# A two-layer cross-attention kernel: the second layer walks the batches backwards, and three pieces of its set-up stand in another order

## The chip, the cores and the metric

One Trainium2 chip, one NeuronCore. The metric is the device time of one execution in microseconds. The engines are TensorE (PE in the rows; its weight loads are PEld), VectorE (DVE), ScalarE (ACT), GpSimd (POOL) and the queue of SyncE (SP), which issues nearly all DMAs. ACT issues a few too.

## The reference

Two cross-attention layers with residuals and an MLP, on x of 8 batches x 56 rows x 256 features. Both layers attend to the same context, 8 batches x 1500 positions x 256.

```python
B, Q, T, D, H, K, F = 8, 56, 1500, 256, 16, 128, 1024

def cross_attention(q_in, kv_in, wq, bq, wk, bk, wv, bv, wo, bo, bias_k, bias_v):
    qh = (q_in @ wq + bq).reshape(b, q_len, H, K)
    kh = (kv_in @ wk + bk).reshape(b, t, H, K)
    vh = (kv_in @ wv + bv).reshape(b, t, H, K)
    kh = concatenate([kh, broadcast(bias_k)], axis=1)   # one more key
    vh = concatenate([vh, broadcast(bias_v)], axis=1)
    weights = softmax(einsum("bqhk,bthk->bhqt", qh, kh) / sqrt(K))
    return einsum("bhqt,bthk->bqhk", weights, vh).reshape(b, q_len, H * K) @ wo + bo

x = x + cross_attention(layer_norm(x, ln1), ctx, ...layer 1...)
x = x + cross_attention(layer_norm(x, ln2), ctx, ...layer 2...)
h = layer_norm(x, ln_mlp)
return x + gelu(h @ w_fc1 + b_fc1) @ w_fc2 + b_fc2
```

## The kernel before

The key projection is moved onto the queries: instead of projecting 12,000 context rows for every head, each head's query is carried through its key weights, so that scores are a product of the context itself with `qt` (256 features, 448 rows x 16 heads). In the same way the softmax weights are applied to the context, and only the result goes through the value and output weights. The one extra key is handled by its own logit (`lb`), for which the "key-bias product" of a head, `g_prod`, multiplies its key weights with the difference `dk` of bias_k and bk, and a reduce sums it into `g_cols`.

Matmuls run on fp32r operands, each split into a high part and a low part (the difference of the value and its high part); a product is three matmuls, high x high, high x low, low x high. So everything that enters a matmul is split first: ACT or DVE makes the high part by a copy, GpSimd or DVE the low part by a subtraction. This holds for the weights (`w_raw` to `w`: `weight_hi` on ACT, `weight_lo` on GpSimd) and for the context: one batch of it is resident in `ctx`, once as rows (`nat`) and once transposed (`tr`), in 4 pieces each. A piece comes by DMA into `nat_stage` or `tr_stage`; `nat_part_hi` and `tr_part_hi` (DVE) and `nat_part_lo` and `tr_part_lo` (GpSimd) split it.

A layer has these stages:

1. Query stage, a loop over 16 heads in quads of four. For head h TensorE computes the query from the normalized rows (L650), ACT copies it out (`query_hi`, L955), DVE takes the difference (`query_lo`, L1222), TensorE carries it through the key weights (L671), ACT writes it to `qt` (L967). Four weight buffers rotate; SP's `load_weight` for head h+4 waits until DVE's product of head h has read its buffer (`gp_ready`) and GpSimd has made its low part. In the same loop the four pieces of batch 0's `nat` and `tr` are loaded and split.
2. Attention stage, a loop over 8 batches. Each batch has two groups (4 and 3 tiles of 128 rows and heads) of 12 chunks of 125 positions: scores (L682), running maximum, shift, exp, split of the weights (L509), weighted context (L703 to L705), with the pieces of the next batch loaded and split as those of this one are used up.
3. Output stage, again a loop over 16 heads: value weights (L650), the extra key's share (a mask `pm` on GpSimd, L568, and L727), output weights (L747). Its input `oth`, the context result of one head, is copied from `qt` in two parts for the first two heads: an early one for the tiles that are complete, a late one (`EARLY`, 3 tiles) for those of the last group.

Then the layer norm of the sum (`norm`: statistics, a chain of small steps from `ln_v` on, `xn`, transposes on TensorE, `ht`).

Every engine has its program written out by hand, in order, with semaphores between the engines. An instruction whose wait is not met holds all that stand behind it on its engine. The order around the change is thus the order of the code in each engine's block. At the start, SP sends `hrow` (rows for the key bias), the four row groups of x, the tables; after DVE's `hdiff`, the difference of two of these rows, it writes `dk_rows` to memory, sends `vrow`, two weight tiles and some tables, and then reads `dk_rows` back, spread over all partitions, as `dk_first` (heads 0 to 3) and `dk_rest`. ACT's queue sends the first two weight tiles.

Semaphore counts that run on over both layers are written as a multiple of the layer, for pieces `l * (B * PIECES)`.

## Time and profile before

| | |
|---|---|
| runs | 1279.06, 1282.16, 2014.25 us; median 1282.16 |
| profiled execution | 1280.71 us, span of its instructions 1278.9 us |
| mean granted TensorE clock | 0.996 |
| busy: TensorE, GpSimd, ScalarE, VectorE | 1252.2, 905.1, 807.2, 794.6 us |
| moved by DMA | 72.58 MB |

The span runs from the first to the last instruction of the core; 1.8 us of the execution lie around it. One of the three runs took much longer than the others. Busy times of engines overlap, so they don't add up to the span. A row of the timeline gives start, duration, engine, line, operation, the written tile, the read ones, shapes and count, and in brackets how long the engine stood idle before it and what ended that. Rows with a count merge several instructions.

### The profile page before, as it was taken

What the parts mean: (1) busy time and instruction counts of PE and PEld (TensorE: products, weight loads), DVE (VectorE), ACT (ScalarE), POOL (GpSimd) and SP (SyncE); (2) the same over time, 40 slices, a digit from 0 to 9 for tenths busy, and PEclk for the clock granted to TensorE, in tenths of its full rate; (3) what the DMA queues carried; (4) which work ended last, traced back from release to release, by engine and by line L of the source; (5) the groups of instructions that cost most, each with busy time, mean ns of one, the idle gap of its engine ahead of it and who ended that gap; (6) DMA issues with size and microseconds to landing.
All of it is one profiled execution on the core that took longest, in us unless ns stands there. A gap on an engine that the chain in (4) does not pass through costs nothing.

```text
span 1278.9 us, 26549 instructions
## 1 busy us (share of the span) xinstructions
PE 1252.2 (98%) x8140; PEld 1152.3 (90%) x8140; DVE 794.6 (62%) x1369; ACT 807.2 (63%) x1585; POOL 905.1 (71%) x750
## 2 busy tenths in 40 slices
PE   6999999999999999999999999999999999999998
PEld 6779999999999999998887999999999999999897
DVE  5745656566666666566785656666656666655654
ACT  4745666666656566676584656666666666666755
POOL 4737777777777777678673768686868686866882
PEclk9999999999999999999999999999999999999999
DMA  5401111111111111012331111111111111101131
GB/s 166 144 10 49 37 61 36 60 36 60 36 60 36 60 37 59 31 39 83 121 126 40 38 38 61 36 60 36 60 36 60 36 60 37 60 30 52 50 95 40
DMA packets 30670, 72.58 MB, mean 57 GB/s; under 512 B 3104, under 2 KB 4512, under 8 KB 30624
## 3 DMA queue, kind: packets, MB, share of 16 engines
q1 hardware_dynamic: 30336, 71.49, 18.1%
q8 instruction: 23, 0.38, 0.1%
q10 hardware_dynamic: 288, 0.52, 0.1%
q14 instruction: 23, 0.19, 0.0%
HBM read 71.52 MB, written 0.48 MB: 56 GB/s over the span
## 4 chain that ended last, share of the span: by engine, by line
PE 91%; DVE 4%; ACT 2%; issue 2%; DMA 0%; POOL 0%; DVEq 0%; ACTq 0%; SPq 0%; POOLq 0%
PE psum L682 36%; PE psum L703 13%; PE psum L704 13%; PE psum L705 13%; PE psum L650 5%; PE psum L747 4%; PE psum L714 2%; PE psum L671 2%; DVE g_prod L1193 1%; PE psum L689 1%; PE psum L696 1%; PE psum L600 1%; DVE qh L1222 1%; ACT on L994 1%; DMA w_raw<-weights 0%
## 5 line engine op out<-in xcount | busy, mean ns | idle before, releaser
L509 POOL TENSOR_TENSOR pt<-slots,pt 125x512 fp32r<-125x512 f32 (+1 forms) x384 | 446.4, 1168 | 216.5 <-ACT slots L988 184.9
L682 PE MATMUL psum<-qs,ctx 128*125 128x384 f32 (+1 forms) x2304 | 543.1, 372 | 1.3 <-ACT slots L1019 0.8
L682 PEld LDWEIGHTS psum<-qs,ctx 128*125 128x125 f32 x2304 | 396.4, 187 | 47.5 <-ACT slots L1019 8.3
L703 PE MATMUL psum<-ctx,pt 125*128 125x258 f32 x1344 | 385.5, 287 | 2.8 <-ACT on L994 2.7
L704 PE MATMUL psum<-ctx,pt 125*128 125x256 f32 x1344 | 379.3, 282 | 0.0
L705 PE MATMUL psum<-ctx,pt 125*128 125x258 f32 x1344 | 379.1, 282 | 0.0
L1281 DVE TENSOR_TENSOR t_max<-psum,t_max 125x512 f32<-125x512 f32 (+1 forms) x320 | 199.2, 622 | 261.2 <-PE psum L682 260.9
L987 ACT ACTIVATE pt<-slots 125x512 fp32r<-125x512 f32 (+1 forms) x384 | 221.1, 576 | 193.1 <-DVE slots L1269 178.6
L1019 ACT ACTIVATE slots<-psum 125x512 f32<-125x512 f32 (+1 forms) x384 | 207.0, 540 | 141.8 <-DVE t_max L1281 132.2
L703 PEld LDWEIGHTS psum<-ctx,pt 125*128 125x128 f32 x1344 | 253.4, 189 | 19.9 <-ACT on L994 12.7
L704 PEld LDWEIGHTS psum<-ctx,pt 125*128 125x128 f32 x1344 | 254.1, 189 | 6.0
L705 PEld LDWEIGHTS psum<-ctx,pt 125*128 125x128 f32 x1344 | 254.6, 189 | 0.0
L1269 DVE TENSOR_TENSOR slots<-slots,psum 125x512 f32<-125x512 f32 (+1 forms) x384 | 232.9, 611 | 19.2 <-PE psum L696 18.1
L988 ACT ACTIVATE slots<-slots 125x512 f32<-125x512 f32 (+1 forms) x384 | 216.7, 564 | 0.0
L446 POOL TENSOR_TENSOR w<-w_raw,w 128x512 fp32r<-128x512 f32 x72 | 106.3, 1482 | 54.9 <-ACT w L929 44.6
L455 POOL TENSOR_TENSOR ctx<-nat_stage,ctx 125x768 fp32r<-125x768 f32 (+1 forms) x64 | 113.5, 1773 | 13.3 <-DVE ctx L1157 12.6
L462 POOL TENSOR_TENSOR ctx<-tr_stage,ctx 128x750 fp32r<-128x750 f32 (+1 forms) x64 | 107.4, 1678 | 19.2 <-DVE ctx L1163 19.2
L470 POOL TENSOR_TENSOR qs<-qt,qs 128x384 fp32r<-128x384 f32 (+1 forms) x60 | 68.8, 1147 | 11.5 <-POOL qs L467 11.5
L1163 DVE CAST ctx<-tr_stage 128x750 fp32r<-128x750 f32 (+1 forms) x64 | 69.0, 1079 | 2.2 <-DMA tr_stage<-ctx_tr 2.2
L1157 DVE CAST ctx<-nat_stage 125x768 fp32r<-125x768 f32 (+1 forms) x64 | 60.4, 944 | 7.1 <-DMA nat_stage<-ctx_nat 6.2
L747 PE MATMUL psum<-w,cs 128*112 128x256 f32 x480 | 62.8, 282 | 1.1 <-DVE cs L1374 1.1
L747 PEld LDWEIGHTS psum<-w,cs 128*112 128x112 f32 x480 | 60.6, 176 | 3.3 <-DVE cs L1374 1.7
(104 smaller groups left out, 1062.2 us busy)
## 6 DMA issues: line engine op xcount, KB each, us to landing
nat_stage<-ctx_nat SPq DMA_DIRECT2D x64, 375.0 KB
tr_stage<-ctx_tr SPq DMA_DIRECT2D x64, 375.0 KB, 3.0
w_raw<-weights SPq DMA_DIRECT2D x70, 256.0 KB, 2.7
dk_rest<-dk_rows SPq DMA_DIRECT2D x2, 768.0 KB, 6.3
w_raw<-weights ACTq DMA_DIRECT2D x2, 256.0 KB, 4.2
dk_first<-dk_rows SPq DMA_DIRECT2D x2, 256.0 KB, 4.5
xres<-x_rows SPq DMA_DIRECT2D x4, 112.0 KB, 4.3
out_rows<-xres SPq DMA_DIRECT2D x4, 112.0 KB, 1.9
```

What stands on the lines that cost most here:

```text
L455: nc.gpsimd.tensor_tensor(lo_part, nat_stage[:], as_f32(hi_part), ALU.subtract).then_inc(nat_lo, 1)
L509: nc.gpsimd.tensor_tensor(split_weights(h, LO, c), slot(h, c), as_f32(split_weights(h, HI, c)), ALU.subtract).then_inc(pt_lo, 1)
L682: last = mm(scores(h, k), ctx_tr_chunk(half, a, c), qs[h][:, m, half, 0:R], start=(half, a, m) == terms[0], stop=(half, a, m) == terms[-1])
L703: mm(out_bank[:, 0:D + 2], hi, ctx_nat_hi(c), start=(c == 0), stop=False, skip_group_check=True)
L704: mm(out_bank[:, 0:D], hi, ctx_nat_lo(c), start=False, stop=False, skip_group_check=True)
L705: return mm(out_bank[:, 0:D + 2], lo, ctx_nat_hi(c), start=False, stop=(c == NCT - 1), skip_group_check=True)
L747: last = mm(Y_BANK[g][0:RGP, 0:D], cs[u][:, a, rows], w[u][:, m, D:2 * D], start=first and (a, m) == (HI, HI), stop=last_head and (a, m) = ...
L987: go(split_weights(h, HI, c), slot(h, c), ACT.Exp)
L988: go(slot(h, c), slot(h, c), ACT.Exp).then_inc(exp_done, 1)
L1019: go(slot(h, c), scores(h, k), ACT.Copy).then_inc(copied, 1)
L1269: V.tensor_tensor(slot(h, c), slot(h, c), shift(h), ALU.subtract).then_inc(sub_done, 1)
L1281: V.tensor_tensor(t_max[h][:], scores(h, k), before, ALU.max).then_inc(max_done, 1)
```

## The change

- Layer 2 takes the batches in the order 7 to 0 (`batch_at`). Batch 7 is the last that layer 1 leaves in `ctx`, so layer 2's query stage neither loads nor splits a batch. The counts of pieces become `l * KEPT` with `KEPT = (B - 1) * PIECES`.
- In layer 2 the last batch is batch 0, so the late part of `oth` covers its 7 tiles (before 3).
- Row groups 0 and 1 of x are the first DMAs of SP's queue, 2 and 3 the first of ACT's. `hrow` follows on SP, and `hdiff` stands behind the second statistics on DVE. ACT's first two weight copies no longer wait for the tables.
- `dv` (the value bias difference) moves into the norm, ahead of the wait for the transposes.
- In layer 1 the key-bias products of heads 0 and 1 stand ahead of the first two query differences, those of heads 2 and 3 right behind them.
- In both output stages ACT copies the weights of head 4 ahead of the results of head 2; the first quad is written out ahead of the loop.

```diff
-EARLY = NT - GT[1]
+KEPT = (B - 1) * PIECES
...
+        def batch_at(l, b):
+
+            return b if l == 0 else b * -1 + (B - 1)
...
+            for g in range(2):
+                sp.dma_start(xres[:, g], x_rows[:, g]).then_inc(x_in[g], 16)
             sp.dma_start(hrow[:], head_rows).then_inc(hrow_in, 16)
-            for g in range(RG):
-                sp.dma_start(xres[:, g], x_rows[:, g]).then_inc(x_in[g], 16)
...
                         load_weight(l * JOBS + quad * 4 + (u + 4), u, l * H + quad * 4 + (u + 1))
-                        if u == 0:
-                            load_nat(0, l * (B * PIECES) + quad, quad)
-                        if u == 2:
-                            load_tr(0, l * (B * PIECES) + quad, quad)
+                        if l == 0 and u == 0:
+                            load_nat(0, l * KEPT + quad, quad)
+                        if l == 0 and u == 2:
+                            load_tr(0, l * KEPT + quad, quad)
...
                     if not last:
-                        load_tr(b + 1, tr, 0)
+                        load_tr(batch_at(l, b + 1), tr, 0)
...
                         weight_lo(l * JOBS + quad * 4 + (u + 4), u)
-                        if u == 1:
-                            nat_part_lo(l * (B * PIECES) + quad, quad)
-                    tr_part_lo(l * (B * PIECES) + quad, quad)
+                        if l == 0 and u == 1:
+                            nat_part_lo(quad, quad)
+                    if l == 0:
+                        tr_part_lo(quad, quad)
...
+            for g in range(2, RG):
+                act.dma_start(xres[:, g], x_rows[:, g]).then_inc(x_in[g], 16)
             for u in range(2):
                 act.dma_start(w_raw[u][:], weights[u]).then_inc(w_in[u], 16)
...
-            act.wait_ge(tables_in, 16 * N_TABLES)
             for u in range(4):
                 act.wait_ge(w_in[u], 16)
                 go(w[u][:, HI, :], w_raw[u][:], ACT.Copy).then_inc(w_hi, 1)
                 if u == 1:
+                    act.wait_ge(tables_in, 16 * N_TABLES)
                     norm(0)
...
+                early, late = (slice(0, NT - GT[1]), slice(NT - GT[1], NT)) if l == 0 else (slice(TILES, NT), slice(0, TILES))
                 for s in range(2):
-                    go(by_tile(oth[s][:, HI])[:, :, 0:EARLY], head_rows_of(s)[:, :, 0:EARLY],
+                    go(by_tile(oth[s][:, HI])[:, :, early], head_rows_of(s)[:, :, early],
                        ACT.Copy).then_inc(oth_early, 1)
...
-                def output_quad(quad, last_quad):
+                def output_quad(quad, first_quad, last_quad):
                     for u in range(4):
+                        if first_quad and u == 0:
+                            weight_hi(l * JOBS + (H + 4), 0, l * 8 + 5)
                         if not (last_quad and u >= 2):
                             head_context((u + 2) % 4, quad * 4 + (u + 2))
                         if not last_quad:
                             context_hi(quad * 4 + (u + 4), u % 2, l * H + quad * 4 + (u + 3))
-                        weight_hi(l * JOBS + quad * 4 + (H + 4 + u), u, l * 8 + quad + 5)
+                        if not (first_quad and u == 0):
+                            weight_hi(l * JOBS + quad * 4 + (H + 4 + u), u, l * 8 + quad + 5)
...
-            dve.wait_ge(hrow_in, 16)
-            V.tensor_tensor(hdiff[:], hrow[:, 0], hrow[:, 1], ALU.subtract).then_inc(dk_ready, 1)
             for g in range(RG):
                 dve.wait_ge(x_in[g], 16)
                 statistics(0, g)
+                if g == 1:
+                    dve.wait_ge(hrow_in, 16)
+                    V.tensor_tensor(hdiff[:], hrow[:, 0], hrow[:, 1], ALU.subtract).then_inc(dk_ready, 1)
                 aggregate(0, g)
...
-                        if u == 1:
-                            nat_part_hi(l * (B * PIECES) + quad, quad)
-                        if u == 3:
-                            tr_part_hi(l * (B * PIECES) + quad, quad)
-
+                        if l == 0 and u == 1:
+                            nat_part_hi(quad, quad)
+                        if l == 0 and u == 3:
+                            tr_part_hi(quad, quad)
+
+                if l == 0:
+                    dve.wait_ge(dk_first_in, 16)
+                    for u in range(2):
+                        key_bias_product(l, u, u, 0, True)
                 query_lo(0, 0)
                 query_lo(1, 1)
                 if l == 0:
-                    dve.wait_ge(dk_first_in, 16)
-                    for u in range(2):
+                    for u in range(2, 4):
                         key_bias_product(l, u, u, 0, True)
```

The order of instructions shows the moves. First VectorE in layer 1, from the end of the norm to the first query differences; `ht` is the normalized input, `qh_10x` the query of head x, `w_raw_92` to `w_raw_95` the four weight buffers. Before:

```order
L1143 TENSOR_TENSOR ht<-ht_118,ht 128x448 x2
L1216 TENSOR_TENSOR dv<-vrow 80x256
L1222 SCALAR_TENSOR_TENSOR qh_100<-psum,col,qh_100 128x448
L1222 SCALAR_TENSOR_TENSOR qh_101<-psum,col,qh_101 128x448
L1193 TENSOR_TENSOR g_prod_80<-w_raw_92,dk_first 128x256
L1197 TENSOR_REDUCE g_cols<-g_prod_80 128x2
L1193 TENSOR_TENSOR g_prod_81<-w_raw_93,dk_first 128x256
L1197 TENSOR_REDUCE g_cols<-g_prod_81 128x2
L1193 TENSOR_TENSOR g_prod_80<-w_raw_94,dk_first 128x256
L1197 TENSOR_REDUCE g_cols<-g_prod_80 128x2
L1222 SCALAR_TENSOR_TENSOR qh_102<-psum,col,qh_102 128x448
L1193 TENSOR_TENSOR g_prod_81<-w_raw_95,dk_first 128x256
```

And now:

```order
L1159 TENSOR_TENSOR ht<-ht_118,ht 128x448 x2
L1209 TENSOR_TENSOR g_prod_80<-w_raw_92,dk_first 128x256
L1213 TENSOR_REDUCE g_cols<-g_prod_80 128x2
L1209 TENSOR_TENSOR g_prod_81<-w_raw_93,dk_first 128x256
L1213 TENSOR_REDUCE g_cols<-g_prod_81 128x2
L1242 SCALAR_TENSOR_TENSOR qh_100<-psum,col,qh_100 128x448
L1242 SCALAR_TENSOR_TENSOR qh_101<-psum,col,qh_101 128x448
L1209 TENSOR_TENSOR g_prod_80<-w_raw_94,dk_first 128x256
L1213 TENSOR_REDUCE g_cols<-g_prod_80 128x2
L1209 TENSOR_TENSOR g_prod_81<-w_raw_95,dk_first 128x256
L1213 TENSOR_REDUCE g_cols<-g_prod_81 128x2
L1242 SCALAR_TENSOR_TENSOR qh_102<-psum,col,qh_102 128x448
```

The two products of heads 0 and 1 moved ahead of their query differences, that of head 3 ahead of head 2's, and `dv` is gone from here.

Then ScalarE where an output stage begins: `cs` is a head's result, `oth` the input of the head two further on, `w_96` the weights of head 4. Before, from the results of head 1 on (the loop begins behind the second row):

```order
L1060 ACTIVATE cs_106<-psum,col 128x448
L1055 ACTIVATE oth_114<-qt 128x896
L1075 UNCONDITIONAL_BRANCH
L1075 ISA
L1060 ISA
L1060 ACTIVATE cs_107<-psum,col 128x448
L1055 ISA
L1055 ACTIVATE oth_113<-qt 128x896
L927 ISA
L928 REGISTER_ALU
L929 ACTIVATE w_96<-w_raw_92 128x512
```

And now:

```order
L1071 ACTIVATE cs_106<-psum,col 128x448
L1066 ACTIVATE oth_114<-qt 128x896
L936 ACTIVATE w_96<-w_raw_92 128x512
L1071 ACTIVATE cs_107<-psum,col 128x448
L1066 ACTIVATE oth_113<-qt 128x896
```

The weights' copy moved ahead of head 2's result and the input of head 4.

Last VectorE in layer 2's query stage, the second half of a quad in the loop. Before:

```order
L1222 SCALAR_TENSOR_TENSOR qh_100<-psum,col,qh_100 128x448
L1193 ISA
L1193 TENSOR_TENSOR g_prod_81<-w_raw_93,dk_rest 128x256
L1196 REGISTER_ALU
L1197 ISA
L1197 TENSOR_REDUCE g_cols<-g_prod_81 128x2
L1163 ISA
L1163 COPY ctx<-tr_stage 128x2x375
L1248 REGISTER_ALU
L1248 COMPARE_AND_BRANCH
```

And now:

```order
L1242 SCALAR_TENSOR_TENSOR qh_100<-psum,col,qh_100 128x448
L1209 ISA
L1209 TENSOR_TENSOR g_prod_81<-w_raw_93,dk_rest 128x256
L1212 REGISTER_ALU
L1213 ISA
L1213 TENSOR_REDUCE g_cols<-g_prod_81 128x2
L1268 REGISTER_ALU
L1268 COMPARE_AND_BRANCH
```

The split of the context piece is gone, and with it, on GpSimd and SP, its low part and its load.

## Rows read from the trace of the kernel before

**Rows 1.** The page: busy times, and the group of one kind of split

```profile
PE 1252.2 (98%) x8140; PEld 1152.3 (90%) x8140; DVE 794.6 (62%) x1369; ACT 807.2 (63%) x1585; POOL 905.1 (71%) x750
...
L1163 DVE CAST ctx<-tr_stage 128x750 fp32r<-128x750 f32 (+1 forms) x64 | 69.0, 1079 | 2.2 <-DMA tr_stage<-ctx_tr 2.2
```

**Rows 2.** Stretches: us, busy PE, PEld, DVE, ACT, POOL, clock, DMA share, GB/s

```profile
64.30:577.00 512.70, 510.81 (x3399) 474.54 (x3400) 315.87 (x552) 325.86 (x660) 368.49 (x312) 1.00 0.14 44
636.30:680.00 43.70, 42.65 (x194) 35.01 (x195) 35.30 (x52) 32.10 (x59) 30.63 (x21) 1.00 0.39 125
```

**Rows 3.** Timeline of the start: start, us, engine, line, operation

```profile
5.03 0.43 DVE L1107 BATCH_NORM_STATS2 ln_stat<-xres 112x6 f32<-112x256 f32 x1 [0.64 <-DMA xres<-x_rows]
...
7.85 0.17 DVE L1118 TENSOR_SCALAR ln_v<-ln_mv 112x4 f32<-112x4 f32 x1
...
8.62 0.35 SPq L350 DMA_DIRECT2D dk_first<-dk_rows  x1
...
15.25 2.54 POOL L446 TENSOR_TENSOR w<-w_raw,w 128x512 fp32r<-128x512 f32 x2 [1.22 <-DVE ht L1143]
...
16.70 1.27 DVE L1222 SCALAR_TENSOR_TENSOR qh<-psum,col,qh 128x448 fp32r<-128x448 f32 x2 [1.32 <-ACT qh L955]
```

**Rows 4.** DMA issues of the first 35 us: KB each, us to landing

```profile
dk_first<-dk_rows SPq DMA_DIRECT2D x1, 256.0 KB, 5.3
...
xres<-x_rows SPq DMA_DIRECT2D x4, 112.0 KB, 4.3
...
hrow<-head_rows SPq DMA_DIRECT2D x1, 48.0 KB, 3.0
```

**Rows 5.** Timeline of layer 1's query stage, its first heads

```profile
17.89 0.41 DVE L1193 TENSOR_TENSOR g_prod<-w_raw,dk_first 128x256 f32<-128x256 f32 x1
17.93 2.59 PE L671 MATMUL psum<-qh,w 128*128 128x448 f32 x12
18.34 0.42 DVE L1197 TENSOR_REDUCE g_cols<-g_prod 128x2 f32<-128x256 f32 x1
18.57 0.35 SPq L339 DMA_DIRECT2D w_raw<-weights  x1
...
21.20 0.63 ACT L929 ACTIVATE w<-w_raw 128x512 fp32r<-128x512 f32 x1 [1.22 <-DMA w_raw<-weights]
...
23.22 1.46 PE L671 MATMUL psum<-qh,w 128*128 128x448 f32 x6 [1.48 <-ACT qt L967]
...
26.16 0.63 ACT L929 ACTIVATE w<-w_raw 128x512 fp32r<-128x512 f32 x1 [2.94 <-DMA w_raw<-weights]
...
28.18 1.47 PE L671 MATMUL psum<-qh,w 128*128 128x448 f32 x6 [2.29 <-ACT qt L967]
```

**Rows 6.** Timeline of layer 2's query stage

```profile
648.46 1.38 PE L650 MATMUL psum<-ht,w 128*128 128x448 f32 x6
...
650.89 1.38 PE L650 MATMUL psum<-ht,w 128*128 128x448 f32 x6
...
657.39 1.65 POOL L455 TENSOR_TENSOR ctx<-nat_stage,ctx 125x768 f32 x1 [0.28 <-issue]
657.54 1.78 DVE L1193 TENSOR_TENSOR g_prod<-w_raw,dk_rest 128x256 f32<-128x256 f32 x1
...
674.74 1.38 PE L650 MATMUL psum<-ht,w 128*128 128x448 f32 x6
```

**Rows 7.** Waits of TensorE from 30 to 62: us in total, times, longest

```profile
PE psum L671 <- ACT qt L967: 1.8, 2, 1.2
```

**Rows 8.** Entry of an output stage: timeline, and TensorE's waits of the whole span

```profile
582.96 3.62 POOL L568 TENSOR_TENSOR pm<-p,mask 80x448 fp32r<-80x448 f32 x2
...
588.25 1.69 POOL L446 TENSOR_TENSOR w<-w_raw,w 128x512 fp32r<-128x512 f32 x1 [1.68 <-ACT w L929]
...
PE psum L650 <- POOL w L446: 2.2, 2, 1.2
...
PE psum L727 <- POOL pm L568: 0.5, 2, 0.3
```

97 lines of the change are left out of this document (51 added, 46 removed).

## The prediction, made before the changed kernel was run

> **What bounds the kernel now.** I read the busy times first. TensorE is busy for 98% of the span [rows 1], so only time in which it stands still, or work added to it, can move the end. Then I cut the span into stages. In an attention stage TensorE is busy for 510.81 of 512.70 us [rows 2]; there are two of them, and the change leaves the matmuls of both as they are. What is left lies in the start, in the two query stages (about 17 to 62 and 637 to 681 us) and where the two output stages begin. There I read the timeline, for what TensorE waited on and what that had waited on.
>
> **Rows of x first.** Before, the bias rows go out first and x behind them, while ACT's queue sends two weight tiles. The first statistics start at 5.03, the step behind the fourth at 7.85 [rows 3]. A copy of x takes 4.3 us to land, the small one in front 3.0 [rows 4]. Now the first copy of x goes out where the small one did (0.76), with no bytes ahead of it. It can land from 0.76+3.0=3.8 to 0.76+4.3=5.1; I take 4.1, nearer the quick row, since half a megabyte of weights now stands behind x. From there I keep the 2.8 us of before (7.85-5.03): hdiff, 0.4, comes in, and takes the place of the wait for the second copy. That gives about 7.0, so **0.8 us** (0 to 1.2). DMA: Bandwidth & Descriptors of the Trainium skill (Issuing engines are not separate DMA queues) says that copies issued by several engines run on the same 16 DMA engines and save issue time only. By that rule alone x would land at its old 4.3 and this term be near 0; the kernel before has two queues filled at once too, so its trace can't tell order from queue.
>
> **Key-bias products ahead.** Here a chain costs more than the start does. SP may ask for head 4's weights only when the first product has read their buffer: product at 17.89, request at 18.57, ACT's copy at 21.20 after 1.22 of waiting. ACT works in order, so the query of head 2 stands behind it, and TensorE waits 1.48 at 23.22. The same for the next head: ACT waits 2.94 at 26.16, TensorE 2.29 at 28.18 [rows 5]. That is 3.8 us in all. Now the first two products stand ahead of the two query differences, those of heads 2 and 3 right behind.
> What it costs hangs on dk_first. It was requested at 8.62 [rows 3] and took 5.3 [rows 4], was there at 13.9, and nobody waited. Before, hdiff ended 0.64 ahead of 5.03, at 4.4; now it stands behind two statistics and ends near 5.6. SP's row of copies behind dk_ready shifts by that 1.2, and dk_first lands at 15.1. DVE is free for it at 14.3 (before just ahead of 15.25, less 0.8; the dv step went into a wait ahead of the transposes' results). From 14.45 GpSimd is in its weight differences, 2.54 for two [rows 3]. How these two meet is shown in layer 2: GpSimd runs from 657.39 to 659.04, and the product that started at 657.54 lasts 1.78 [rows 6], where one alone lasts 0.41 [rows 5]; it ends 0.28 after GpSimd does. SBUF — State Buffer of the Trainium skill (Who interferes with whom) says that a VectorE instruction with two SBUF inputs and a GpSimd one that reads SBUF shut each other out, and that a reduce does not contend; the trace agrees, and the rule speaks against this part of the change.
> So product 0 waits for GpSimd's first and ends at 15.9, product 1 for its second and ends at 17.5, the reduce takes 0.42 [rows 5] and head 0's query difference 0.65 [rows 3]: TensorE takes head 0 at 18.6, 0.7 later than the 17.93 of before. But head 4's weights are asked for at 16.2. ACT comes to them 2.05 after TensorE starts on head 0 (before 21.20-1.22=19.98 against 17.93), at 20.65, and finds them. Head 2 went 2.0 after that copy began (21.20 to 23.22), now at 22.7. Head 5's weights landed at 26.1, crowded by what was asked for right behind them, 7.6 after head 4's request; 6.5 after 16.2 would be 22.7, when ACT comes, and the products of heads 2 and 3 now let the requests behind them follow 2 us later. Head 3 then goes 2.4 after head 2, at 25.1 instead of 28.18. Gain at this point, x included: **3.0 us**. With dk_first in time, head 0 goes at 17.2 and head 3 at 23.6: 4.6. With dk_first 2 later than I say: 1.0. From there each load keeps its distance, so the two later waits of this stage, 1.8 us [rows 7], for weights behind a context copy, I leave: 0 (to 1.8).
>
> **Output entry.** TensorE stands 2.2 us in two waits, one in each layer, for GpSimd's weight difference of head 4, and 0.5 for the mask behind it [rows 8]. That difference starts at 588.25, after waiting 1.68 for ACT's copy, which ACT had in order behind the results of head 2. The copy's own condition, that head 0's rows are out, is met before GpSimd is free at 582.96+3.62=586.58. Put ahead, it lets the difference run from 586.6 to 588.3; TensorE is ready at 588.8 (589.99 less the wait of 1.2). Both waits go: **2.7 us** (1.2 to 2.8; the low end if a difference of VectorE stands in GpSimd's way, as at 582.96, where two masks took 3.62). In layer 2 the last two copies of oth grow from 48 to 112 elements a partition, small beside the pick matmuls that run there: 0 (to -0.2).
>
> **Layer 2 keeps the last split.** Gone are 8 copies of 375 KB, 8 VectorE and 8 GpSimd steps. TensorE takes a head every 2.43 when nothing is late (648.46 to 650.89); but from 648.46 to 674.74 ten heads take 26.28 where ten times 2.43 is 24.3 [rows 6]: 2.0 too long. VectorE is late: a head needs a query difference of 0.65, a product of 0.41 to 1.8 and a reduce of 0.42, and twice in four heads a split of about 1.08 [rows 1] on top. Without the splits the worst head is 0.65+1.8+0.42=2.9, once, and GpSimd, busy 30.63 of 43.70 [rows 2], loses eight steps of about 1.65, 13, so most products miss it. **2.0 us** (1.0 to 2.9, the high end if the heads ahead of 648 gain too). The first transposed piece of batch 6 is now free to be fetched early; nobody waits for it.
> Reversing the batches leaves the loop bodies as long as they were, give or take a register step, and in 512.70 us only 1.9 are not covered by matmuls. ACT's output loops have their first round written out: more code to fetch, 0 (to -0.5).
>
> **Sum.** 3.0+0+2.7+2.0-0.1=7.6. The profiled execution took 1280.71 with a span of 1278.9; 1.8 lie around it. It stands between the quickest run shown (1279.06) and the median (1282.16). **1280.7-7.6=1273.1 us.** All low ends give 2.5 (1278.2), all high ends 12.1 (1268.6).
>
> **Rivals.**
> Heads 0 and 1 pay for it: dk_first lands 2 later than 15.1, behind the two weight tiles and the tables that SP sends first. For it: it is last in that row, and took 5.3 where a copy of x took 4.3. Against: only 1.2 has moved. The start then gives 1.0: 1275.1.
> Layer 2's query stage keeps its pace, since something else is late there, ACT or a product beside a weight difference. For it: the product of 1.78. Against: 2.43 is reached with all of ACT's work in it. 2.0 less: 1275.1.
> It gives more: the later waits of layer 1 (1.8) go as well, as GpSimd and the loads are no longer behind there, and dk_first is 0.7 earlier: 1270.6.
> Slower than before: dk_first comes so late that VectorE, in order behind it, holds all queries, then TensorE. Each us that it lands after 15.1 costs one, and the 7.6 are gone when it lands after 22.7, 13 after its request, more than twice the 5.3. At 25 the time is 1283. For it only that the write to memory ahead of it now starts 1.2 later and is waited for; against, the row has nothing of that size.
> The change does not do what it says: TensorE's waits are replaced one for one by others that the ones of before hid. Then 1280.
>
> **Chances.** Forecast 0.62, heads 0 and 1 pay 0.13, layer 2 keeps its pace 0.10, more 0.10, nothing 0.03, slower 0.02. The range, 1267.0 to 1279.0, takes in the first four with the ends of their terms. 2% (26 us, about what a measurement of this kernel can tell from no change) is outside all of them: faster 0.01, within 0.97, slower 0.02.
>
> **What would show it.** The first statistics near 4.1, the step behind the fourth at 7.0. A product of 1 us or more beside GpSimd's differences at 15 to 17, and TensorE at head 0 some 0.7 later than 17.93. No wait of ACT for the weights of heads 4 and 5, and head 3 at 25. In layer 2 2.43 between heads, its query stage 41.7 long instead of 43.7. No wait for GpSimd at head 4 in either output stage. Attention stages within 0.5 of 512.7. I am wrong if dk_first holds VectorE beyond 17, if a wait for ACT stands in layer 2 where VectorE's stood, or if the attention stages move.

## The result, and the profile after

| | before | after |
|---|---|---|
| median of the runs, us | 1281.51 (6 runs, from 1279.06) | 1274.67 (6 runs, 1272.87 to 1276.37) |
| ratio | | 0.9952, 95% interval 0.9938 to 0.9966 |
| profiled execution, span | 1278.9 | 1272.5 |
| mean granted clock | 0.996 | 0.997 |
| moved by DMA | 72.58 MB | 69.50 MB |

The changed kernel takes 6.2 us less (4.4 to 7.9); 1273.1 was forecast. By the bound of 2% that is no change, but it is more than the measurement is uncertain. One execution each of the kernel before (2014.25), of e1 (2440.1) and of e4 (1500.2) ran far longer than the rest and is left out of the ratios. The line numbers of the changed kernel are some 6 to 20 higher: L650 of before is L657, L671 is L678, L703 is L710, L747 is L754, L1193 is L1209, L1222 is L1242.

To see where the 6.4 us between the two spans come from I cut both traces at the same events: the first score matmul of each attention stage, the first matmul of each output stage (it reads oth), and the first transpose of the layer norm behind it. "Query 2" runs from that transpose to the next attention stage. The same table for the twelve kernels of the next section stands here too. All lengths are as they stand in the traces, in us. * marks a query 2 or an attention 2 with a stretch at half clock in it, which costs an attention stage about 1.5 (see the last section), so starred values are to be compared with starred ones.

| kernel | attention 1 starts | output 1 | query 2 | attention 2 | output 2 | ratio to before (95%) |
|---|---|---|---|---|---|---|
| before | 64.30 | 55.34 | 49.15 | 513.72* | 54.23 | |
| after | 60.49 | 53.80 | 47.20 | 514.72* | 53.83 | 0.9952 (0.9938-0.9966) |
| e1 | 65.14 | 55.35 | 49.17 | 512.11 | 54.26 | 0.9998 (0.9988-1.0009) |
| e2 | 60.43 | 55.36 | 50.29* | 511.95 | 54.27 | 0.9970 (0.9956-0.9984) |
| e3 | 62.82 | 55.37 | 47.19 | 513.04 | 54.38 | 0.9986 (0.9977-0.9995) |
| e4 | 63.35 | 54.82 | 50.34* | 512.01 | 53.69 | 0.9989 (0.9978-0.9999) |
| e5 | 59.61 | 53.82 | 47.18 | 513.68 | 53.83 | 0.9962 (0.9949-0.9976) |
| e6 | 60.12 | 53.83 | 47.20 | 514.42* | 53.83 | 0.9952 (0.9935-0.9968) |
| e7 | 60.71 | 54.16 | 47.18 | 514.48* | 53.16 | 0.9957 (0.9940-0.9973) |
| e8 | 59.11 | 54.13 | 48.17* | 514.81* | 53.15 | 0.9950 (0.9935-0.9966) |
| e9 | 61.79 | 54.81 | 47.78 | 512.26 | 53.80 | 0.9943 (0.9930-0.9956) |
| e10 | 59.44 | 54.09 | 48.17* | 513.74* | 53.15 | 0.9935 (0.9923-0.9948) |
| e11 | 61.23 | 53.78 | 47.17 | 514.57* | 53.85 | 0.9963 (0.9950-0.9977) |
| e12 | 63.41 | 54.83 | 47.75 | 513.07 | 53.87 | 0.9978 (0.9969-0.9988) |

From before to after: 3.81 are gained ahead of attention 1, 0.06 in it, 1.54 in output 1, 1.95 in query 2; 1.00 is lost in attention 2 (513.72 to 514.72, with a half-clock stretch in each); 0.40 is gained in output 2, and 0.31 is lost behind it (the last 28.20 us become 28.51). That sums to 6.45. The first figure is the least firm: e3 and e4 have the start of the kernel before and reach attention 1 at 62.82 and 63.35, so about 1 of the 3.81 is that this trace of the kernel before was a late one.

The page, where [rows 1] stood for before. TensorE's busy time falls by 2.5, since what goes is mostly waiting; 4 of the splits of transposed pieces are gone.

```profile
PE 1249.7 (98%) x8140; PEld 1151.3 (90%) x8140; DVE 783.6 (62%) x1361; ACT 808.8 (64%) x1585; POOL 891.3 (70%) x742
...
L1179 DVE CAST ctx<-tr_stage 128x750 fp32r<-128x750 f32 (+1 forms) x60 | 65.0, 1084 | 1.1 <-DMA tr_stage<-ctx_tr 1.1
```

The stretches, as [rows 2]. The two attention stages do the same work, yet in the second TensorE is busy for 1.07 less of an equal stretch; in the kernel before the two differ by 0.16 (510.81 and 510.65). The second row is the window of [rows 2] between the same events: 41.74 instead of 43.70, with GpSimd busy for 16.76 (before 30.63) and VectorE for 22.97 (before 35.30).

```profile
60.49:573.19 512.70, 510.74 (x3400) 474.56 (x3400) 315.37 (x552) 326.03 (x660) 368.53 (x312) 1.00 0.14 44
630.90:672.64 41.74, 41.22 (x194) 35.48 (x195) 22.97 (x44) 32.31 (x59) 16.76 (x13) 1.00 0.27 75
675.40:1188.10 512.70, 509.67 (x3394) 473.83 (x3395) 314.20 (x552) 326.06 (x660) 367.63 (x311) 1.00 0.14 44
```

The start, as [rows 3] and [rows 5]. The columns are start, duration, engine, line, operation, and in brackets the idle time and its releaser.

```profile
3.98 0.43 DVE L1122 BATCH_NORM_STATS2 ln_stat<-xres 112x6 f32<-112x256 f32 x1 [2.96 <-DMA xres<-x_rows]
...
6.42 0.17 DVE L1133 TENSOR_SCALAR ln_v<-ln_mv 112x4 f32<-112x4 f32 x1
...
9.46 0.35 SPq L354 DMA_DIRECT2D dk_first<-dk_rows  x1
...
13.84 2.71 POOL L451 TENSOR_TENSOR w<-w_raw,w 128x512 fp32r<-128x512 f32 x2 [1.22 <-DVE ht L1159]
...
14.80 0.59 DVE L1209 TENSOR_TENSOR g_prod<-w_raw,dk_first 128x256 f32<-128x256 f32 x1 [1.17 <-DMA dk_first<-dk_rows]
...
15.65 0.35 SPq L343 DMA_DIRECT2D w_raw<-weights  x1
15.76 1.07 DVE L1209 TENSOR_TENSOR g_prod<-w_raw,dk_first 128x256 f32<-128x256 f32 x1
...
18.02 2.67 PE L678 MATMUL psum<-qh,w 128*128 128x448 f32 x12 [1.36 <-DVE qh L1242]
...
22.12 1.45 PE L678 MATMUL psum<-qh,w 128*128 128x448 f32 x6 [0.22 <-ACT qt L976]
...
25.18 1.47 PE L678 MATMUL psum<-qh,w 128*128 128x448 f32 x6 [0.40 <-ACT qt L976]
```

The first statistics come 1.05 earlier and ln_v 1.43. Then VectorE stands 1.17 for dk_first, asked for at 9.46 and there at 14.8; its second product runs beside GpSimd's difference and takes 1.07. TensorE takes head 0 at 18.02, not earlier than before (17.93), and 0.8 later than in e1, e3 and e4, where it is 17.20 to 17.23. But head 4's weights are asked for at 15.65 instead of 18.57, and the waits for ACT's results at heads 2 and 3 are 0.22 and 0.40 instead of 1.48 and 2.29. Head 3 goes at 25.18: 3.00 gained against this trace, 2.1 to 2.3 against e3 and e4 (27.32, 27.47). The two later waits of [rows 7] shrink as well, from 0.65 and 1.20 to 0.43 and 0.39.

The query stage of layer 2, as [rows 6]: TensorE takes a head every 2.43 from end to end (643.05 to 667.37 for ten), and the product takes 0.42, with no GpSimd step in its way.

```profile
643.05 1.38 PE L657 MATMUL psum<-ht,w 128*128 128x448 f32 x6
...
645.49 1.38 PE L657 MATMUL psum<-ht,w 128*128 128x448 f32 x6
...
643.41 0.42 DVE L1209 TENSOR_TENSOR g_prod<-w_raw,dk_rest 128x256 f32<-128x256 f32 x1
```

The entries of the output stages, as [rows 8]:

```profile
579.08 1.09 DVE L1391 TENSOR_TENSOR oth<-qt,oth 128x896 fp32r<-128x896 f32 x1 [0.15 <-ACT oth L1066]
...
579.10 3.60 POOL L575 TENSOR_TENSOR pm<-p,mask 80x448 fp32r<-80x448 f32 x2
...
1194.92 1.91 DVE L1391 TENSOR_TENSOR oth<-qt,oth 128x896 fp32r<-128x896 f32 x1 [0.15 <-ACT oth L1066]
...
1197.36 2.47 DVE L1391 TENSOR_TENSOR oth<-qt,oth 128x896 fp32r<-128x896 f32 x1
...
1194.95 2.68 POOL L575 TENSOR_TENSOR pm<-p,mask 80x448 fp32r<-80x448 f32 x2
1197.59 1.28 POOL L451 TENSOR_TENSOR w<-w_raw,w 128x512 fp32r<-128x512 f32 x1
...
1199.88 0.67 PE L657 MATMUL psum<-oth,w 128*128 128x448 f32 x2 [1.14 <-DVE oth L1391]
```

For comparison, VectorE's first difference for oth in the kernel before, in layer 1 and in layer 2:

```profile
582.94 1.09 DVE L1368 TENSOR_TENSOR oth<-qt,oth 128x896 fp32r<-128x896 f32 x1 [0.15 <-ACT oth L1055]
...
1201.15 1.90 DVE L1368 TENSOR_TENSOR oth<-qt,oth 128x896 fp32r<-128x896 f32 x1
```

In the changed kernel no wait of TensorE for GpSimd's weight difference is left, in either layer. In layer 1 VectorE's difference for oth starts at 579.08, GpSimd's masks 0.02 later, and VectorE's takes 1.09. In layer 2 it starts 0.03 ahead too, but there it is VectorE's that is held: it takes 1.91 and the two masks 2.68 instead of 3.60. VectorE's next difference takes 2.47 beside the weight difference, and TensorE waits 1.14 for it.

### The profile page after: what moved, and what is told of

Read it like the earlier page. It is cut to its first block, busy times and chain, and to the rows that moved or that the text cites. A ratio compares the mean times of both kernels' runs of the same rounds, so it can differ in the third digit from the quotient of the medians.

```text
span 1272.5 us, 26437 instructions
## 1 busy us (share of the span) xinstructions
PE 1249.7 (98%) x8140; PEld 1151.3 (90%) x8140; DVE 783.6 (62%) x1361; ACT 808.8 (64%) x1585; POOL 891.3 (70%) x742
## 2 busy tenths in 40 slices
DMA packets 29574, 69.50 MB, mean 55 GB/s; under 512 B 3021, under 2 KB 4429, under 8 KB 29529
## 4 chain that ended last, share of the span: by engine, by line
PE 92%; DVE 3%; ACT 2%; issue 1%; POOL 1%; DMA 0%; SPq 0%; DVEq 0%; ACTq 0%; POOLq 0%
PE psum L689 36%; PE psum L710 13%; PE psum L711 13%; PE psum L712 13%; PE psum L657 5%; PE psum L754 4%; PE psum L678 3%; PE psum L721 2%; PE psum L696 1%; PE psum L703 1%; ACT on L1003 1%; ACT qt L976 1%; DVE g_prod L1209 1%; DMA dk_first<-dk_rows 0%; PE psum L734 0%
## 5 line engine op out<-in xcount | busy, mean ns | idle before, releaser
L710 PE MATMUL psum<-ctx,pt 125*128 125x258 f32 x1344 | 385.0, 286 | 3.8 <-ACT on L1003 3.3
L710 PEld LDWEIGHTS psum<-ctx,pt 125*128 125x128 f32 x1344 | 253.5, 189 | 20.8 <-issue 6.9
L460 POOL TENSOR_TENSOR ctx<-nat_stage,ctx 125x768 fp32r<-125x768 f32 (+1 forms) x60 | 106.4, 1773 | 11.1 <-DVE ctx L1173 10.7
L467 POOL TENSOR_TENSOR ctx<-tr_stage,ctx 128x750 fp32r<-128x750 f32 (+1 forms) x60 | 100.5, 1675 | 17.1 <-DVE ctx L1179 17.1
L1179 DVE CAST ctx<-tr_stage 128x750 fp32r<-128x750 f32 (+1 forms) x60 | 65.0, 1084 | 1.1 <-DMA tr_stage<-ctx_tr 1.1
L472 POOL CAST qs<-qt 128x384 fp32r (+3 forms) x60 | 33.5, 559 | 45.4 <-PE psum L689 45.4
L754 PE MATMUL psum<-w,cs 128*112 128x256 f32 x480 | 62.8, 282 | 1.1 <-DVE cs L1397 1.1
L754 PEld LDWEIGHTS psum<-w,cs 128*112 128x112 f32 x480 | 60.6, 176 | 3.3 <-DVE cs L1397 1.7
```

The costliest lines, as they stand in the source:

```text
L710: mm(out_bank[:, 0:D + 2], hi, ctx_nat_hi(c), start=(c == 0), stop=False, skip_group_check=True)
L754: last = mm(Y_BANK[g][0:RGP, 0:D], cs[u][:, a, rows], w[u][:, m, D:2 * D], start=first and (a, m) == (HI, HI), stop=last_head and (a, m) = ...
```

## The experiments

Each was timed beside the kernel before on the same chip: e1 to e4 on one, e5 to e8 on a second, e9 to e12 on a third. So ratios of different groups are compared with care, and lengths of stages carry most of the argument. How far starts of the same code lie apart sets what can be told there: with the start of the changed kernel, attention 1 begins at 60.49, 59.61 (e5), 60.71 (e7) and 61.79 (e9, with a half-clock stretch at head 1). e1 to e4 put one part of the change into the kernel before.

**e1, rows of x alone.**

```diff
+            for g in range(2):
+                sp.dma_start(xres[:, g], x_rows[:, g]).then_inc(x_in[g], 16)
             sp.dma_start(hrow[:], head_rows).then_inc(hrow_in, 16)
-            for g in range(RG):
...
+            for g in range(2, RG):
+                act.dma_start(xres[:, g], x_rows[:, g]).then_inc(x_in[g], 16)
```

> The kernel before with one part of the change: rows of x lead both queues, the difference of the bias rows stands behind the second statistics, ScalarE's first copies don't wait for the tables, the value bias difference stands in the norm. Theory A (each part of the start carries its own share): the step behind the fourth statistics comes 1.4 earlier, as in the changed kernel (6.42 instead of 7.85), and all of it reaches head 3, since the first product and with it the request for head 4's weights move along: head 3 at 26.7 instead of 28.18, end 1.4 earlier. Theory B (the loads of heads 4 and 5 set head 3, crowded by the other DMAs of the start, whatever comes before): the first heads are 1.4 earlier, head 3 stays at 28.2, end within 0.3 of before.

The ratio is 0.9998. The first transposes stand at 9.50, but in e3 and e4, whose start is that of the kernel before, they stand at 9.77 and 9.73: the 10.45 of the trace before was a late one. Heads 2 and 3 wait 1.62 and 2.58 for the weights of heads 4 and 5, as long as before or longer, and attention 1 starts at 65.14. Head 3 goes at 28.02 (27.32 and 27.47 in e3 and e4). Theory B holds: nothing of the earlier x comes through that these runs could tell. (One stretch at half clock, from 27.6 to 31.0, lies in this start, and makes its 65.14 look worse than it is.)

**e2, the key-bias products alone.**

```diff
+                if l == 0:
+                    dve.wait_ge(dk_first_in, 16)
+                    for u in range(2):
+                        key_bias_product(l, u, u, 0, True)
                 query_lo(0, 0)
                 query_lo(1, 1)
                 if l == 0:
-                    dve.wait_ge(dk_first_in, 16)
-                    for u in range(2):
+                    for u in range(2, 4):
```

> The kernel before with one part of the change: the key-bias products of heads 0 and 1 ahead of their query differences, those of heads 2 and 3 right behind. Theory A: both products stand beside GpSimd's two weight differences (15.25 to 17.8) and are held by them, query differences from 18.2, TensorE takes head 0 at 19.0 (before 17.93), no DMA wait for dk_first; head 4's weights are asked for 2 earlier, head 3 at 26.6 instead of 28.18, and the end comes 1.6 earlier. Theory B (the load queue is crowded, the earlier request lands no earlier): head 0 at 19.0 and head 3 at 28.2 or later, end 0 to 1 later than before.

0.9970, 3.8 less, and attention 1 at 60.43: the same as with the whole change. Here nobody waits for dk_first (asked for at 8.61), and the first product slips in 0.05 behind GpSimd's start without being held; only the second is:

```profile
14.34 3.06 POOL L446 TENSOR_TENSOR w<-w_raw,w 128x512 fp32r<-128x512 f32 x2 [1.22 <-DVE ht L1143]
14.39 0.41 DVE L1193 TENSOR_TENSOR g_prod<-w_raw,dk_first 128x256 f32<-128x256 f32 x1
...
15.17 1.07 DVE L1193 TENSOR_TENSOR g_prod<-w_raw,dk_first 128x256 f32<-128x256 f32 x1
```

TensorE takes head 0 at 17.43, 0.2 later than in e3 and e4, not at the 19.0 that I had expected of both theories. Head 3 goes at 24.69. A for the gain, and more than it had asked for.

**e3, the reversed batches and the kept split alone.** It is the whole change without the three other parts.

> The kernel before with one part of the change: layer 2 walks the batches backwards and its query stage neither loads nor splits a batch; the late part of oth covers 7 tiles there. Theory A (the register step that the reversed index puts ahead of ScalarE's scaled copies of the results costs TensorE 0.06 at each of 14 groups): the query stage of layer 2 is 1.9 shorter, its attention stage 0.9 longer, end 1.0 earlier. Theory B (the longer attention stage of the changed kernel comes from its other parts, or from chance): query stage 1.9 shorter, attention stage as before within 0.2, end 1.9 earlier.

Query 2 takes 47.19 and attention 2 takes 513.04. Without the reversal query 2 takes 49.15 (before, 49.17 in e1), and attention 2 takes 511.95 to 512.11 where no half-clock stretch lies in it, as here (e1, e2, e4). The loss belongs to this part and is no chance. That it is ScalarE's register step is not shown by this. Ratio 0.9986.

**e4, the weights' copy alone.**

```diff
+                        if first_quad and u == 0:
+                            weight_hi(l * JOBS + (H + 4), 0, l * 8 + 5)
                         if not (last_quad and u >= 2):
                             head_context((u + 2) % 4, quad * 4 + (u + 2))
```

> The kernel before with one part of the change: ScalarE copies the weights of head 4 ahead of the results of head 2 in both output stages, with the first quad written out ahead of the loop. Theory A (GpSimd's weight difference was late, and nothing stands behind it): 1.5 in each output stage, 3.0 in all. Theory B (in each layer it hangs on which of VectorE and GpSimd gets in first as the stage begins, a tie of 20 to 30 ns): 1.5 where VectorE's difference for oth starts ahead of GpSimd's mask, 0.4 where behind; the sum is 1.9 if layer 2 falls as in the changed kernel, and VectorE then waits beside the mask.

Neither 1.5 nor a split of 1.5 and 0.4: output 1 gains 0.52 and output 2 0.54, since here GpSimd got in first in both. The wait for the weight difference (1.19 in the kernel before, 1.05 to 1.06 in e1 to e3) becomes one for VectorE of 1.13 that ends 2.1 sooner after the stage begins:

```profile
581.93 1.90 DVE L1372 TENSOR_TENSOR oth<-qt,oth 128x896 fp32r<-128x896 f32 x1 [0.15 <-ACT oth L1055]
...
584.35 2.48 DVE L1372 TENSOR_TENSOR oth<-qt,oth 128x896 fp32r<-128x896 f32 x1
...
581.95 2.67 POOL L568 TENSOR_TENSOR pm<-p,mask 80x448 fp32r<-80x448 f32 x2
...
586.88 0.68 PE L650 MATMUL psum<-oth,w 128*128 128x448 f32 x2 [1.13 <-DVE oth L1372]
```

Theory B by its mechanism. Of ten kernels with this part, counted by VectorE's first row at the entry of output 1, it took 1.09 in four (after, e5, e6, e11: output 1 at 53.8) and 1.90 in three (e4, e9, e12: 54.8); in e7, e8 and e10 the order is forced. In output 2 GpSimd won in all seven. What decides it in output 1 no run shows.

**e5, the reversed index in another place.** den and rden are kept in the order of the walk.

```diff
-                           scale=rden[:, ds(batch_at(l, b) * TILES + (h * GT[0] + j), 1)]).then_inc(on_act, 1)
+                           scale=rden[:, ds(b * TILES + (h * GT[0] + j), 1)]).then_inc(on_act, 1)
...
-                    V.reciprocal(rden[:, at], den[:, at]).then_inc(rden_ready, 1)
+                    V.reciprocal(rden[:, walked], den[:, walked]).then_inc(rden_ready, 1)
```

> The changed kernel, with the sums den and their reciprocals rden kept in the order in which the batches are walked, so that the two engines that scale the results with them need no index of the reversed batch; all else stays. Theory A (the reversed index adds a register step that TensorE waits out at each group, and that is where the 1.0 of layer 2's attention stage went): the waits for the scaled results fall from 1.9 to 1.4, the attention stage is 0.9 to 1.0 shorter, end 1.0 earlier. Theory B (it is the other indices, those of the transposed results and of the extra key, or the loads' other order): the stage keeps its length within 0.2, and so does the end.

Attention 2 takes 513.68, no shorter than the 513.04 of e3, and the wait for the scaled results rises from 1.9 to 2.1. My theory falls: the index is not the cause. It made me look at one group event by event. In the changed kernel (sum of the group, ScalarE's scaled copies, the next group's first context matmul):

```profile
828.70 0.16 DVE L1326 TENSOR_TENSOR den<-psum,p_extra 128x3 f32 x1 [0.52 <-PE psum L712]
...
829.29 0.84 ACT L1003 ACTIVATE on<-psum,rden 128x256 f32<-128x256 f32 x2 [0.58 <-DVE rden L1329]
...
829.91 0.36 PE L710 MATMUL psum<-ctx,pt 125*128 125x258 f32 x1 [0.28 <-ACT on L1003]
```

The sum stands at 828.70, ScalarE's copies 0.59 later, TensorE 1.21 later. In the kernel before the three distances are 0, 0.58 and 1.11 (835.73, 836.31, 836.84). So both engines are on time, and it is TensorE that takes 0.10 more from the same release. In e5 TensorE stands 1.22 behind the sum (824.79 and 826.01), with a wait of 0.31.

**e6, dk_first ahead of three tables.**

```diff
+            sp.wait_ge(dk_written, 16)
+            load_dk_first(0)
             sp.dma_start(mask[:], mask_in).then_inc(consts_in, 16)
             sp.dma_start(pick[:], pick_in).then_inc(consts_in, 16)
             sp.dma_start(spread[:], spread_in).then_inc(consts_in, 16)
-            sp.wait_ge(dk_written, 16)
-            load_dk_first(0)
```

> The changed kernel, with dk_first asked for ahead of three tables of constants in SyncE's queue. Theory A (in the changed kernel VectorE stood 1.17 for it, then ran its products into GpSimd's differences, and this ate what the earlier x gave): request 1.4 earlier at 8.0, product 0 ends before GpSimd starts, head 0 at 16.8 instead of 18.02, and half or more of it reaches the attention stage (59.5 instead of 60.5), end 0.6 to 1.2 earlier. Theory B (the loads of weights and context set the pace from head 2 on): head 0 at 16.8, attention stage at 60.4, end as the changed kernel's.

dk_first is asked for at 8.34 instead of 9.46.

```profile
13.83 0.41 DVE L1209 TENSOR_TENSOR g_prod<-w_raw,dk_first 128x256 f32<-128x256 f32 x1
...
14.11 2.72 POOL L451 TENSOR_TENSOR w<-w_raw,w 128x512 fp32r<-128x512 f32 x2 [1.22 <-DVE ht L1159]
...
14.61 1.05 DVE L1209 TENSOR_TENSOR g_prod<-w_raw,dk_first 128x256 f32<-128x256 f32 x1
```

No wait for dk_first, product 0 is through before GpSimd hurts it, product 1 is held (1.05) as ever. Attention 1 starts at 60.12 with first transposes 0.27 later than in the changed kernel; with the same start in e8 and e10 it starts at 59.11 and 59.44. So 0.4 to 1.4 come through against the changed kernel, of a request that is 1.1 to 1.4 earlier. That points to theory A but doesn't show it: e5, without this edit, starts attention 1 at 59.61, as dk_first happened to be there in time (product 0 at 14.02, head 3 at 24.00; 23.69 to 24.31 with the edit). The ratio, 0.9952, can't tell it from the changed kernel.

**e7, GpSimd's masks behind VectorE's difference.**

```diff
+                pool.wait_ge(oth_lo, INIT + l * H + 3)
                 for u in range(2, 4):
                     mask_extra(u, u - 2, l * H + (u - 1))
```

> The changed kernel, with GpSimd's masks of heads 2 and 3 waiting for VectorE's difference of head 2's input (oth) at the entry of both output stages. Theory A (who gets in first there decides, and GpSimd's row of mask, mask and weight difference holds VectorE's next difference): VectorE's takes 1.09 in both layers, the next 1.2 instead of 2.47, TensorE's wait of 1.14 in layer 2 goes, the output stage of layer 2 is 1.1 shorter, that of layer 1 stays; end 1.1 earlier. Theory B (GpSimd, 0.9 later with its masks, makes TensorE wait for head 4's weights or mask instead): the wait changes its name, end within 0.3 of the changed kernel.

```profile
1195.25 1.09 DVE L1392 TENSOR_TENSOR oth<-qt,oth 128x896 fp32r<-128x896 f32 x1
...
1196.86 1.58 DVE L1392 TENSOR_TENSOR oth<-qt,oth 128x896 fp32r<-128x896 f32 x1
...
1196.55 2.67 POOL L575 TENSOR_TENSOR pm<-p,mask 80x448 fp32r<-80x448 f32 x2 [1.25 <-DVE oth L1392]
```

VectorE's differences take 1.09 and 1.58 (the second gets in between GpSimd's two masks), the wait of 1.14 is gone, output 2 is 0.67 shorter. Output 1 is 0.36 longer, since there the lucky order of the changed kernel (53.80) is replaced by the forced one (54.16), with two small waits of 0.2. 0.3 in all: between the theories, and the price of the tie is now known. Output 1 takes 55.3 before, 54.8 if GpSimd is first, 53.8 if VectorE is, 54.1 if it is forced.

**e8, the three edits of e5, e6 and e7 together.**

> The changed kernel with the three edits of the runs before this one together. Theory A (they lie in three stages and add): 1.0 + 0.9 + 1.1, 3.0 less than the changed kernel, 9.2 less than the kernel before. Theory B for each as before; if all three hold, the end is that of the changed kernel.

0.9950. Attention 1 starts 1.4 earlier, the output stages give 0.35, attention 2 stays at 514.81 (514.72 in the changed kernel, both with a half-clock stretch). Theory A fails for e5's part; the traces are with it, in smaller sizes than expected, for the other two.

**e9, TensorE's thresholds as before.** The counts of low parts go on by 32 a layer for those who wait on them.

```diff
-                        pe.wait_ge(nat_lo, INIT + l * KEPT + b * PIECES + (i // STEPS) * PIECES + c // PCT + 1)
+                        pe.wait_ge(nat_lo, INIT + l * SPLITS + b * PIECES + (i // STEPS) * PIECES + c // PCT + 1)
...
+                else:
+                    nc.gpsimd.memset(count_step[:, 0:4], 0.0).then_inc(nat_lo, PIECES)
+                    nc.gpsimd.memset(count_step[:, 4:8], 0.0).then_inc(tr_lo, PIECES)
```

> The changed kernel, with the counts of low parts (nat_lo, tr_lo) that TensorE and SyncE wait for numbered again as 32 a layer instead of 28: GpSimd adds the missing 4 in two tiny memsets as layer 2's query stage ends. TensorE's row of instructions is then word for word that of the kernel before. Theory A (with 28 a layer TensorE can't share the register that holds the threshold of another semaphore, also 32 a layer, and at the first context product of a group it must first work through one more step when the scaled results are released: 0.10 at each of 13 groups): the first context product starts 1.11 behind the sum of the group instead of 1.21, the waits for the scaled results fall from 1.9 to 1.4, layer 2's attention stage from 513.0 to 512.1 (without a stretch at half clock), end 0.9 earlier. Theory B (ScalarE's or VectorE's index steps or the turned order of loads cost it, by a way that the last runs did not touch): 1.21 and 513.0 stay.

The order of TensorE's instructions ahead of that context matmul in layer 2's loop, before (and in e9):

```
L842 REGISTER_ALU [waits pt_lo]
L703 MATMUL psum<-ctx,pt 128x258 [waits on_act]
```

and in the changed kernel:

```
L842 REGISTER_ALU
L849 EVENT_SEMAPHORE [waits on_act]
L710 MATMUL psum<-ctx,pt 128x258 [waits pt_lo]
```

The traces have this too. At the line where TensorE waits for the scaled results, from 690 to 1185, stand in before, in after, and in e9 (one EVENT_SEMAPHORE ahead of the loop is in all of them and is the fifteenth of after):

```profile
L842 PEldq ALU_OP  x14: 32/32/32, 740.8 to 1150.8; - x14
```

```profile
L849 PEldq EVENT_SEMAPHORE  x15: 51/51/51, 702.5 to 1147.0; - x15
```

```profile
L854 PEldq ALU_OP  x14: 32/32/32, 734.8 to 1144.7; - x14
```

Waits for the scaled results in attention 2, from 690 to 1185 (us in total, times, longest), of before, of after, and of e9:

```profile
PE psum L703 <- ACT on L994: 1.4, 7, 0.3
```

```profile
PE psum L710 <- ACT on L1003: 1.9, 7, 0.3
```

```profile
PE psum L715 <- ACT on L1008: 1.4, 7, 0.3
```

One group of e9:

```profile
829.85 0.16 DVE L1331 TENSOR_TENSOR den<-psum,p_extra 128x3 f32 x1 [0.52 <-PE psum L717]
...
830.96 0.39 PE L715 MATMUL psum<-ctx,pt 125*128 125x258 f32 x1 [0.19 <-ACT on L1008]
```

The distance is 1.11 again, the wait 0.19, the total 1.4, and attention 2 takes 512.26: theory A. Nor does it rest on one trace. Without a half-clock stretch attention 2 takes 511.95 to 512.26 with 32 a layer (e1, e2, e4, e9) and 513.04 to 513.68 with 28 (e3, e5, e12); with one, 513.72 and 513.74 (before, e10) against 514.42 to 514.81 (after, e6, e7, e8, e11). The counts on SP and two memsets on GpSimd are changed by e9 as well, but they stand outside the waits shown here.

The mechanism is one instruction in the way. With 32 a layer a register instruction carries the wait for the weights' low part, which is over early, and the matmul itself the wait for ScalarE's copy: the matmul starts 0.05 behind that copy's end. With 28 an EVENT_SEMAPHORE, an instruction that only waits, stands between the two. In the changed kernel's group shown under e5 it starts at 829.80, 0.04 behind the end of ScalarE's first copy, takes 0.05, and the matmul starts 0.11 after it began, so 0.14 behind the copy. So it stands at all 14 such places of the stage, and at 13 of them the matmul starts 0.09 to 0.10 later than in the kernel before. That would be 1.2 to 1.3; the stage is 0.9 to 1.0 longer, so not all of it comes through. The numbers 32 l + 4 b of nat_lo are those of on_act too (4 of them a batch), and with 28 a layer they no longer are. That the program's instructions came out otherwise for that reason is argued; that they went back with the numbers is shown.

**e10, e6, e7 and e9 together.**

> The changed kernel with the counts as before, dk_first ahead of the constants, and the masks of heads 2 and 3 behind VectorE's difference. Theory A: 0.9 in layer 2's attention stage, 0.7 to 1.4 ahead of the first one, 0.3 in the two output stages: 2.2 less than the changed kernel, 8.5 less than the kernel before. Theory B (attention stage as the changed kernel's): 1.3 less than the changed kernel.

0.9935 (0.9923 to 0.9948), 8.3 less than before: the fastest of all, as A expects. Attention 1 at 59.44, attention 2 at 513.74 (514.72 in the changed kernel, with a half-clock stretch in both), output 2 at 53.15. Its interval overlaps that of the changed kernel, so that the 2 us between the two rest on the traces.

**e11, all of x on one queue.**

> The changed kernel, with all four row groups of x first on SyncE's queue instead of two there and two on ScalarE's. Theory A (the order in a queue is what counts, a second queue saves issue time only): first statistics at 4.0, the fourth 0 to 0.4 later than in the changed kernel, first transposes at 9.0 to 9.4, attention stage and end within 0.4. Theory B (the second queue brings data sooner, and the weights on ScalarE's queue now land ahead of the later rows of x): first transposes at 10 or later, end 0.5 to 1 later.

```profile
5.21 0.43 DVE L1120 BATCH_NORM_STATS2 ln_stat<-xres 112x6 f32<-112x256 f32 x1 [0.42 <-DMA xres<-x_rows]
...
7.27 0.38 DVE L1120 BATCH_NORM_STATS2 ln_stat<-xres 112x6 f32<-112x256 f32 x1
```

The second statistics wait 0.42 more for their copy, and the third start at 7.27 (5.26 in the changed kernel), because VectorE stands in between for hrow, which now goes out behind four copies. So the run doesn't part order from queue: the first copy lands at the same time (4.14 against 3.98), the rest is the wait for hrow. But it shows something else. The transposes come 2.0 later than in the changed kernel (11.03), and attention 1 only 0.74 (61.23), which is within what starts of the same code differ by. This start hardly hangs on x.

DMA: Bandwidth & Descriptors of the Trainium skill (Issuing engines are not separate DMA queues) says that a second issuing engine saves issue time only. No run here decides it; that the landing of the first copy is the same by either way agrees with it.

**e12, the products back in their place.**

> The changed kernel, with the key-bias products in their old place behind the query differences; all else stays, x too. Theory A (the products carry all that the start gains, and the earlier x gives nothing by itself, because the weights of heads 4 and 5 come late either way): first attention stage at 63 to 65 instead of 60.5, TensorE waits 1.5 and 2.5 at heads 2 and 3, end 3.5 later than the changed kernel. Theory B (the earlier x and the products each carry a part): 61.5 to 62.5, end 1 to 2 later.

Starts of ScalarE's copies for heads 4 and 5, and TensorE's waits at heads 2 and 3:

```profile
20.46 0.63 ACT L936 ACTIVATE w<-w_raw 128x512 fp32r<-128x512 f32 x1 [1.41 <-DMA w_raw<-weights]
...
25.90 0.63 ACT L936 ACTIVATE w<-w_raw 128x512 fp32r<-128x512 f32 x1 [3.42 <-DMA w_raw<-weights]
...
22.47 1.45 PE L678 MATMUL psum<-qh,w 128*128 128x448 f32 x6 [1.66 <-ACT qt L976]
...
27.91 1.48 PE L678 MATMUL psum<-qh,w 128*128 128x448 f32 x6 [2.77 <-ACT qt L976]
```

Attention 1 at 63.41, 2.9 later, ratio 0.9978, 3.3 us more than by the changed kernel's: theory A. It is also where e3 and e4 are (62.82, 63.35), which have neither the earlier x nor the products. The x that leads both queues is there in this kernel, and ends as a longer wait for the weights of heads 4 and 5 (1.41, 3.42; before 1.22, 2.94).

## Why the prediction was right, and where it was not

It said 1273.1, 1.6 under the median measured, and 7.6 gained where the spans show 6.4. Term by term:

- **Rows of x, 0.8.** The step behind the fourth statistics came 1.43 earlier. But 0.7 to 0.9 of that was a late landing in the trace before (7.85; 6.95 to 7.18 in e2, e3, e4). What I had not seen is that it is worth nothing that can be told at attention 1 (e1, e12, and 60.43 without it in e2 against 60.49 with it). The sum holds only because I had counted x inside the chain to head 3.
- **Chain to head 3, 3.0.** Measured 3.00, and head 3 at 25.18 for 25.1. That it fits to 0.1 is partly luck: 0.7 to 0.9 of the 3.00 is the late trace before, and by e3 and e4 as the measure it is 2.1 to 2.3. Head 2 went at 22.12 (22.7), head 0 at 18.02 (18.6), since product 0 took 0.59 and not the length of a GpSimd difference. That head 0 pays 0.7 holds against the 17.2 of e1, e3 and e4. dk_first landed at 14.8 (15.1). The cause is the one given: the earlier request for head 4's weights (e2 alone has it all, e12 loses it). The rival in which heads 0 and 1 pay did not come.
- **Later waits of layer 1, 0 (to 1.8).** They gave 0.8: the rival "it gives more", in part.
- **Output entry, 2.7 (1.2 to 2.8).** 1.54 in layer 1, 0.40 in layer 2 (0.55 without the longer late part of oth, e3). The wait for GpSimd went in both, as forecast. The step that failed is "TensorE is ready at 588.8": in layer 2 it is not, as VectorE's next difference is then late behind GpSimd's row of mask, mask and weight difference. I had the low end "if a difference of VectorE stands in GpSimd's way"; it is the other way round. The profile before showed it: VectorE's difference took 1.09 in layer 1 and 1.90 in layer 2, in the same place. It cost nothing there, as TensorE waited longer for the weight difference (1.19 and 1.05).
- **Query stage of layer 2, 2.0.** 1.95, 2.43 a head, 47.2.
- **Reversal 0 (to -0.5), attention stages within 0.5.** This failed. Attention 2 is 1.0 longer, more than the bound. I had written "I am wrong if [...] the attention stages move", and for this step I am. "Give or take a register step, and in 512.70 us only 1.9 are not covered" was the wrong reading: 1.4 of those 1.9 are seven waits of TensorE for a scaled result, and at such a place every tenth that it takes to react counts, as at the groups where the trace shows it busy till then (0.10 more at these too). e9 shows that the cost lies in TensorE's own waits, which changed with the counts of pieces (one EVENT_SEMAPHORE more at each), and not in the walk. The term that was put at nothing is the new count of pieces.
- **The last 0.31.** In the changed kernel and in all with 28 a layer the span goes on 0.3 longer behind the last layer norm (28.45 to 28.56), in e9 and e10 it doesn't (28.17, 28.15). The work itself ends at the same distance (25.91 before and after). What differs is GpSimd's last two semaphore instructions, with which the engines finish together (L83): they stand 0.08 apart in before (1278.72, 1278.80), e1, e2, e4, e9 and e10, and 0.38 in after (1271.98, 1272.36) and the rest. Why is open.

Two errors, 0.8 more ahead of attention 1 (3.81 for 3.0) and 0.8 less in the output entry (1.94 for 2.7), nearly cancelled, which is luck, and the first of them is for the most part the late start of the trace before; what remains of the difference is attention 2 and the tail. A time that comes out within 1.6 was worth less as evidence than the list of stages.

## What to carry to other kernels

Where a load waits for the reader of its buffer, put that reader first: 3 us came from two short products moved ahead of the work that looked more urgent, and nothing that twelve runs could tell from starting the program's first input earlier. When a count that others wait on changes by a constant, compare each engine's instructions at the few places where the bound engine really waits; one more instruction between a release and a matmul that stands still for it showed as 0.1 each time. And judge parts of a few us by the lengths of stages between the same events, not by the end: starts and half-clock stretches move that by as much.
